# Two 64-row tiles for the first projection, earlier input of the next quad, and a new written order in a conv, attention and Fourier network

## The reference

```
# conv(x), twice, with its own weights each time:
r  = sigmoid(mean_over_positions(x) @ Wr + br)         # 4 mixing weights per image
h  = relu(bn1(x @ sum_e r_e Wpw_e + ...))              # 24 -> 96 channels
h  = relu(bn2(depthwise_3x3(h, sum_e r_e Wdw_e) + ...))
x  = bn3(h @ sum_e r_e Wpwl_e + ...) + x               # 96 -> 24
# then on tokens, each with a layer norm over channels before it:
t += linear_attention(ln(t))                           # no softmax: q (k^T v)
t += ffn(ln(t))                                        # operands rounded to fp8, sums to f16
t += fourier_layer(ln(t))                              # 24 -> 48, fft over tokens, per-channel mix, relu, ifft, 48 -> 24
t += ffn(ln(t))
```

## Time and profile before

| | us |
|---|---|
| median of 3 runs (lowest, highest) | 2447.91 (2443.51, 2450.33) |
| profiled execution | 2448.76 |
| its span | 2447.0 |
| mean granted TensorE clock | 0.903 |

### The profile page before, as it was taken

One profiled execution on the slowest core, in us unless ns is written; L12 is line 12 of the kernel. 1 busy time (PEld: TensorE's weight loads), 2 busy tenths in 40 slices (PEclk: granted clock), 3 DMA queues, 4 the chain that ended last, 5 costly groups with the idle time before them and its releaser, 6 DMA issues.

```text
span 2447.0 us, 48861 instructions
## 1 busy us (share of the span) xinstructions
PE 2087.6 (85%) x19720; PEld 1234.5 (50%) x19720; DVE 1924.6 (79%) x3745; ACT 1583.8 (65%) x2704; POOL 114.6 (5%) x290
## 2 busy tenths in 40 slices
PE   3777988999979989999789987898889998887865
PEld 2233433664446634665347634376347644663753
DVE  4986988799949999699959996698978999366253
ACT  3344447775777677765777666776767667767544
POOL 0000000000000000000000000000000000000000
PEclk9887989999979999999989997899999999987765
DMA  5001000100020000100020002000010000000000
GB/s 147 1 1 21 1 1 5 18 2 1 1 40 2 2 1 15 28 2 1 1 40 2 2 1 41 1 2 1 1 32 2 2 1 1 22 2 1 21 1 20
DMA packets 108591, 29.62 MB, mean 12 GB/s; under 512 B 104144, under 2 KB 104272, under 8 KB 107984
## 3 DMA queue, kind: packets, MB, share of 16 engines
q1 hardware_dynamic: 108368, 26.50, 5.3%
HBM read 16.85 MB, written 9.63 MB: 11 GB/s over the span
## 4 chain that ended last, share of the span: by engine, by line
DVE 40%; PE 36%; ACT 13%; issue 7%; SPq 3%; DMA 1%; ACTq 0%; DVEq 0%
DVE acc L1505 19%; PE P L757 7%; PE P L738 5%; PE P L972 4%; DVE SQ L1670 3%; PE P L1064 3%; SPq L598 3%; DVE arena L1654 3%; PE P L909 2%; DVE arena L1670 2%; PE P L779 2%; DVE roots L1670 2%; PE P L806 2%; PE P L985 2%; DVE T L1521 1%
## 5 line engine op out<-in xcount | busy, mean ns | idle before, releaser
L1505 DVE SCALAR_TENSOR_TENSOR acc<-H,Dm,acc 128x784 f32<-128x784 f32 x1024 | 999.2, 1029 | 30.7 <-ACT acc L1140 30.3
L738 PE MATMUL P<-T,Wk 112*128 112x448 f32 (+1 forms) x768 | 385.7, 593 | 55.7 <-ACT H L1133 32.2
L757 PE MATMUL P<-H,diag 64*64 64x392 f32 x4608 | 404.5, 501 | 15.5 <-DVE T L1521 12.4
L1133 ACT ACTIVATE H<-P,biasA 128x448 f32<-128x448 f32 (+1 forms) x384 | 237.3, 622 | 206.0 <-PE P L738 182.7
L757 PEld LDWEIGHTS P<-H,diag 64*64 64x64 f32 x4608 | 174.9, 135 | 228.7 <-issue 191.1
L738 PEld LDWEIGHTS P<-T,Wk 112*128 112x128 f32 x768 | 130.8, 200 | 172.2 <-ACT H L1133 104.1
L1163 ACT ACTIVATE acc<-P,biasT 128x392 f32<-128x392 f32 x128 | 71.7, 584 | 128.8 <-PE P L757 128.8
L1140 ACT ACTIVATE acc<-H,Dm 128x784 f32<-128x784 f32 x128 | 121.6, 950 | 8.1 <-PE P L779 5.8
L1169 ACT ACTIVATE acc<-acc,biasA 128x784 f32<-128x784 f32 x128 | 118.4, 948 | 10.7 <-DVE acc L1505 10.4
L997 PE MATMUL P<-pack_b,arena 128*96 128x112 f32 x928 | 112.3, 268 | 10.6 <-DVE roots L1670 4.6
L972 PEld LDWEIGHTS P<-pack_b,arena 113*64 113x64 f32 x1792 | 112.7, 216 | 16.8 <-issue 7.6
(11 more groups left out here) (209 smaller groups left out, 3630.0 us busy)
## 6 DMA issues: line engine op xcount, KB each, us to landing
xin<-in_x SPq DMA_DIRECT2D x224, 42.0 KB, 2.3
out_y<-arena SPq DMA_DIRECT2D x8, 1176.0 KB, 6.1
pack_b<-in_pack_b SPq DMA_DIRECT2D x1, 3870.5 KB, 17.5
arena<-in_pack_s SPq DMA_DIRECT2D x1, 1584.0 KB, 8.6
pack_a<-in_pack_a SPq DMA_DIRECT2D x1, 1084.0 KB, 5.3
pack_i<-in_pack_i SPq DMA_DIRECT2D x1, 320.0 KB, 3.2
arena<-in_pack_k SPq DMA_DIRECT2D x1, 192.0 KB, 3.4
```

The costliest lines, as they stand in the source:

```text
L738: pe.matmul(conv_rows(slice(0, 128), HB[(NP * s + e) % len(HB)], n), Wk1[:, 128 * j:128 * (j + 1)], image_rows(T[q % 3], a, n), start=True ...
L757: last = pe.matmul(conv_rows(slice(64 * h, 64 * (h + 1)), CVB + r, HH), diag[64 * r:64 * (r + 1), tap, :], H1[64 * r:64 * (r + 1), slot(s, ...
L1133: act.activation(H1[:, slot(s, j), o:o + n, 1:1 + HW], conv_rows(slice(0, 128), HB[(NP * s + e) % len(HB)], n), ACT.Relu, bias=biasA[:, j, ...
L1505: ins = ve.scalar_tensor_tensor(a, H1[:, slot(s, j), r:r + SR, c:c + HW], Dm[:, j, tap:tap + 1], a, ALU.mult, ALU.add)
```

## The change

Seven edits:
1. `hidden`: tile 0 takes only rows 0 to 63 of the contraction (images 0 and 1) and tile 2 only rows 64 to 111 (images 2 and 3); the rows left out are zero in the weights. Both matmuls of a pair are issued in one step and write two banks. Tile 1 keeps all 112 rows. The pieces are taken in the order tile 0, tile 2 (8 rows each), tile 0, tile 2 (the rest), tile 1.
2. Banks: hidden pieces, and the input of quads after the first, have banks 0 and 5. Back has 6 and 7 left, the router's result is in bank 0.
3. There are four T buffers, so the copy to T waits for the output of quad q - 4.
4. The input's sums have a tile of their own (`part_in`), and the input transposes no longer wait for the end of the quad before; they wait for its `h1_ready`. The wait for that end now stands on DVE before the mixing of the weights.
5. The first quad's input groups 4 to 6 are loaded ahead of the packs "s" and "b".
6. PE's taps of a strip are three steps, not one.
7. All strings of `TURNS` are new. POOL waits for its own last memset in middle, and a scratch for DMAs is halved.

```diff
--- before.py
+++ after.py
 TURNS = {
...
     "tensor": (
-        "c15 d1 c9 d1 c4 d3 c2 m1 c2 d4 c1 d3 c9 d1 c8 d3 m1 c1 d1 c1 d1 c3 m1 c2 m1 d2 c1 m1 d1 m1 d1 m3 d1 "
...
+        "c13 d1 c1 d1 c1 d1 c3 d2 c1 d2 c1 d1 c2 d1 c2 d2 c1 d9 c5 d1 c1 d1 c2 d1 c3 d1 c1 m1 d1 c1 m1 d4 c2 "
...
     "scalar": (
-        "c8 m1 c9 d1 c1 d1 c7 d1 c1 d1 c2 d2 c2 d1 c3 d1 c5 d4 c2 d4 c14 d1 c3 d3 c2 d2 c5 d2 m1 c8 d4 m2 c1 "
...
+        "c19 d1 c3 d1 c1 d2 c2 d1 c3 d1 c3 d1 c1 d1 c4 d2 c3 d2 c1 d4 c1 m1 c15 d2 c2 d1 c2 d1 c2 m1 c1 d2 c2 "
...
     "vector": (
-        "c3 m1 c20 d1 c2 d1 c18 d1 c2 d1 c12 d2 c10 d2 c23 d2 c16 d1 c3 d1 c13 d1 c2 d1 c10 d2 m1 c1 m2 c2 m4 "
...
+        "c22 d2 c18 d2 c16 d1 c1 d1 c10 d2 c3 m1 c21 d2 c14 d2 c17 d2 c12 d2 c2 m1 c1 m6 c1 m1 c25 d1 c2 d1 c3 "
...
-    XG = 4
-    MB, CB = (3, 4), (0, 1, 2)
+    XG, TB = 4, 4
+    MB, CB, HB = (3, 4), (0, 1, 2, 5), (0, 5)
...
-    BB = (5, 6, 7)
+    BB = (6, 7)
...
+    def input_banks(q):
+
+        return CB if q == 0 else HB
+
     def hidden_banks(q, L):
 
-        return CB[:1] if q > 0 else CB[:1] + MB + BB if L == 0 else CB[:1] + BB
+        return HB if q > 0 else HB + MB + BB if L == 0 else HB + BB
...
-        Ts = [sb(f"T{n}", [R, TOK]) for n in range(3)]
+        Ts = [sb(f"T{n}", [R, TOK]) for n in range(TB)]
...
-        part = sb("part", [R, 8])
+        part, part_in = sb("part", [R, 2 * NS]), sb("part_in", [R, NCK])
...
+        LGB, CVB = 0, 1
 
...
-        pieces = ((0, 0), (0, 1), (2, 0), (2, 1), (TJ, 0), (TJ, 1))
+        pieces = ((0, 0), (2, 0), (0, 1), (2, 1), (TJ, 0), (TJ, 1))
...
                 sp.dma_start(pack_t[key], packs[key]).then_inc(par_loaded[key].sem, 16)
             load(0, range(XG))
-            for key in ("a", "s", "b"):
+            sp.dma_start(pack_t["a"], packs["a"]).then_inc(par_loaded["a"].sem, 16)
+            load(0, range(XG, NCK))
+            for key in ("s", "b"):
                 sp.dma_start(pack_t[key], packs[key]).then_inc(par_loaded[key].sem, 16)
             for q in range(NQ):
-                load(q, range(XG, NCK))
+                if q > 0:
+                    load(q, range(XG, NCK))
                 if q + 1 < NQ:
                     load(q + 1, range(XG))
...
                 pool_e.memset(bdw[2][:, 0:MR], 0.0).then_inc(ones_ready.sem, 1)
+                pool_e.wait_ge(ones_ready.sem, ones_ready.at(q, 2))
                 yield from shift_terms(q, normM, 1)
...
                     if g == 0 and not first(q):
-                        pe.wait_ge(cv_added.sem, cv_added.at(q, 0))
-                    if g >= 3:
-                        pe.wait_ge(in_evac.sem, in_evac.at(q, g - 2))
+                        pe.wait_ge(h1_ready.sem, h1_ready.at(q, 0))
+                    if g >= len(IB):
+                        pe.wait_ge(in_evac.sem, in_evac.at(q, g - len(IB) + 1))
                     for s in range(BPG):
                         o = RC * (BPG * (n % XG) + s)
-                        last = pe.transpose(P[0:R, g % 3, BLK * s:BLK * (s + 1)], xin[:, o:o + R], par["ident"][0:BLK, 0:BLK])
+                        last = pe.transpose(P[0:R, IB[g % len(IB)], BLK * s:BLK * (s + 1)], xin[:, o:o + R], par["ident"][0:BLK, 0:BLK])
                     last.then_inc(in_tp.sem, 1)
...
                 last.then_inc(lg_psum.sem, 1)
 
             def hidden(q, L):
-                HB = hidden_banks(q, L)
+                banks = hidden_banks(q, L)
                 for s in range(NS):
                     for e, (j, k) in enumerate(pieces):
                         a, n, _ = piece_rows(s, k)
-                        yield
-                        if s == 0 and e == 0:
-                            pe.wait_ge(cw_ready.sem, cw_ready.at(q, L + 1))
-                        else:
-                            pe.wait_ge(h1_ready.sem, h1_ready.at(q, max(NP * L * NS, NP * (L * NS + s) + e + 1 - len(HB))))
-                        pe.matmul(conv_rows(slice(0, 128), HB[(NP * s + e) % len(HB)], n), Wk1[:, 128 * j:128 * (j + 1)],
-                                  image_rows(T[q % 3], a, n), start=True, stop=True).then_inc(h1_psum.sem, 1)
+                        pair = j != TJ
+                        if not pair or j == 0:
+                            yield
+                            if s == 0 and e == 0:
+                                pe.wait_ge(cw_ready.sem, cw_ready.at(q, L + 1))
+                            else:
+                                pe.wait_ge(h1_ready.sem, h1_ready.at(q, max(NP * L * NS, NP * (L * NS + s) + e + 1 + pair - len(banks))))
+                        rows = slice(32 * j, 32 * j + 64 - 8 * j) if pair else slice(0, R)
+                        pe.matmul(conv_rows(slice(0, 128), banks[(NP * s + e) % len(banks)], n), Wk1[rows, 128 * j:128 * (j + 1)],
+                                  image_rows(T[q % TB][rows, :], a, n), start=True, stop=True).then_inc(h1_psum.sem, 1)
...
                 for tap in range(NTAP):
                     dy, dx = tap // 3, tap % 3
+                    if tap and dx == 0:
+                        yield
                     for r in range(2):
                         for h in range(2):
                             last = pe.matmul(conv_rows(slice(64 * h, 64 * (h + 1)), CVB + r, HH), diag[64 * r:64 * (r + 1), tap, :],
...
+                IB = input_banks(q)
                 for g in range(NCK):
                     yield
-                    if g == 0 and q >= 3:
-                        act.wait_ge(ot_psum.sem, ot_psum.at(q - 2, 0))
+                    if g == 0 and q >= TB:
+                        act.wait_ge(ot_psum.sem, ot_psum.at(q - TB + 1, 0))
                     act.wait_ge(in_tp.sem, in_tp.at(q, g + 1))
-                    act.activation(by_token_block(T[q % 3])[:, BPG * g:BPG * (g + 1), :],
-                                   P[0:R, g % 3, 0:CK].rearrange("p (s n) -> p s n", s=BPG),
-                                   ACT.Copy, accum_out=part[:, g:g + 1]).then_inc(in_evac.sem, 1)
...
-                link(ve.tensor_reduce(pool[:, :], part[:, 0:(NCK if L == 0 else 2 * NS)], AX.X, ALU.add), q, "conv")
+                link(ve.tensor_reduce(pool[:, :], part_in[:, :] if L == 0 else part[:, :], AX.X, ALU.add), q, "conv")
...
                 yield
                 ve.wait_ge(rw_ready.sem, rw_ready.at(q, L + 1))
+                if L == 0 and not first(q):
+                    ve.wait_ge(cv_added.sem, cv_added.at(q, 0))
 
...
```

More of the change, by code:

```diff
@@ L422, in build @@
         P = ctx.enter_context(nc.psum_tensor("P", [128, 8, 512], F32))
-        LGB, CVB = 2, 1
+        LGB, CVB = 0, 1
         def image_rows(t, r0, n):
@@ L806, in layer_norm @@
                         pe.matmul(P[0:R, cen[c % NC], 0:CK], par["cen"][0:R, :],
-                                  T[q % 3][:, CK * c:CK * (c + 1)], start=True, stop=True).then_inc(norm.cen_psum.sem, 1)
+                                  T[q % TB][:, CK * c:CK * (c + 1)], start=True, stop=True).then_inc(norm.cen_psum.sem, 1)
                     if c >= 1:
@@ L1063, in output_transposes @@
                     for s in range(BPG):
-                        last = pe.matmul(P[0:BLK, FB[g % BN], RC * s:RC * (s + 1)], by_token_block(T[q % 3])[:, BPG * g + s, :],
+                        last = pe.matmul(P[0:BLK, FB[g % BN], RC * s:RC * (s + 1)], by_token_block(T[q % TB])[:, BPG * g + s, :],
                                          par["rest"][0:R, :], start=True, stop=True)
@@ L1108, in copy_in @@
             def copy_in(q):
+                IB = input_banks(q)
                 for g in range(NCK):
                     yield
-                    if g == 0 and q >= 3:
-                        act.wait_ge(ot_psum.sem, ot_psum.at(q - 2, 0))
+                    if g == 0 and q >= TB:
+                        act.wait_ge(ot_psum.sem, ot_psum.at(q - TB + 1, 0))
                     act.wait_ge(in_tp.sem, in_tp.at(q, g + 1))
-                    act.activation(by_token_block(T[q % 3])[:, BPG * g:BPG * (g + 1), :],
-                                   P[0:R, g % 3, 0:CK].rearrange("p (s n) -> p s n", s=BPG),
-                                   ACT.Copy, accum_out=part[:, g:g + 1]).then_inc(in_evac.sem, 1)
+                    act.activation(by_token_block(T[q % TB])[:, BPG * g:BPG * (g + 1), :],
+                                   P[0:R, IB[g % len(IB)], 0:CK].rearrange("p (s n) -> p s n", s=BPG),
+                                   ACT.Copy, accum_out=part_in[:, g:g + 1]).then_inc(in_evac.sem, 1)
             def conv(q, L):
-                HB = hidden_banks(q, L)
+                banks = hidden_banks(q, L)
                 yield
@@ L1132, in relu1 @@
                         act.wait_ge(acc_ready.sem, acc_ready.at(q, L * NV + 2 * (s - 2) + j // 2 + 1))
-                    act.activation(H1[:, slot(s, j), o:o + n, 1:1 + HW], conv_rows(slice(0, 128), HB[(NP * s + e) % len(HB)], n), ACT.Relu,
+                    act.activation(H1[:, slot(s, j), o:o + n, 1:1 + HW], conv_rows(slice(0, 128), banks[(NP * s + e) % len(banks)], n), ACT.Relu,
```

(12 more changed lines are left out.)

## The result

The changed kernel takes 2414.1 us (median of four, 2404.5 to 2420.7), the kernel before 2449.1 us in the same session: ratio 0.986, 95% interval 0.982 to 0.990. That is 35 us faster, where 75 were forecast. The profiled execution took 2420.7 us with a span of 2418.8; before, 2448.8 and 2447.0. It was the slowest of the four, so its trace shows 28 of the 35 us; the same kernel was profiled again as after_again, with a span of 2407.7.

A forecast was written before the change was run, and what follows sets the result against it. Bounds: PE full and DVE nearly full in long stretches, conv dependencies at quad changes. From 2448.8 us: start -15, changes of quads -60, pairs -19, order of pieces +4, back's bank +15, giving 2374 us; range 2285 to 2448.

The forecast's parts named there:

- rival 3: Hidden matmul pairs don't run beside each other; PE gains nothing and pays 41 us of shape changes: 2408 us, chance 0.04.
- Rival 1: Quad changes return little, their work only moving into stretches where PE is full; 10 instead of 60: 2424 us, chance 0.16.
- The start, -15: Quad 0's input groups load earlier, the seventh at 19.5 us; saves 15 us, between 7 and 22.
- its 7.9 us: Delay of the first taps by `setup_rest` on DVE, expected to cost the same at the second conv: nothing won or lost.
- The changes of quads, -60: Seven windows, a quad's last add to the next quad's first DVE tap, shrink; 60 us saved, bounds 10 and 109.
- Wrong if the windows shrink and the quads' period does not: Sign that would refute the forecast: shorter windows between quads without a shorter period per quad.
- The pairs, -19: Two 64-row hidden matmuls run beside each other; net 52 us of PE, 0.36 of it counting: 19 us saved (0 to 52).
- the price of broken taps: PE's strip taps split into steps: 77 broken blocks at 0.2 us of shape changes, 15 us of PE.
- The order of pieces, +4: First strip: tile 0's second piece waits for two relus, first centre tap 0.6 us later, seven times: 4 us lost.
- Back's lost bank, +15: Back's ffn down to one hidden bank, its Fourier layer to two banks: 15 us lost, between 0 and 160.
- rival 4: Back's two banks make PE stand 0.3 us per group, 160 us: slower, 2519 us; break-even 0.17 us; chance 0.12.

The follow-up runs named there:

- before_loads: Kernel before with only the new order of loads (quad 0's last three input groups ahead of packs s and b): 2435.5 us, 0.996.
- full_rows: Changed kernel with the outer tiles' first projections on all 112 rows, so no pairs: 2422.7 us, 0.991; with a searched order 2411.8 us.
- The uncoupling with a searched order: Kernel before plus fourth T buffer, part_in, later wait on adds, new loads, three-step taps; old banks, no pairs, order from the second search: 2409.4 us, 0.986.
- replan runs: Orders from the first search, by replay with mean durations: changed kernel 2413.4 us, bank5_drain 2391.1 us, kernel before 2493.6 us.
- order2 runs: Orders from a second search, also counting handovers and shape changes: changed kernel 2397.9 us, bank5_drain 2365.8 us, kernel before 2458.2 us.
- bank5_drain: Changed kernel with bank 5 given back to the back stage of quad 6, beside which no conv runs: 2403.9 us, 0.983.
- after_order2: Changed kernel's code with an order from the second search, counting handovers and shape changes: 2397.9 us, 0.981.
- bank5_order2: bank5_drain with an order from the second search, counting handovers and shape changes: 2365.8 us, 0.967.
- one_tap_step: Changed kernel with a strip's nine taps in one step of PE's order, the two freed steps left empty behind it: 2551.3 us, 1.045.

## Why the prediction was right or wrong

The direction was right, the size wrong: 2414 is inside the range and 40 us above the forecast. By the number it lies between rivals 3 (2408) and 1 (2424); the trace rules out 3, and 1 fits in part.

- **The start, -15.** Right in its mechanism. The seventh group came at 20.7 us (19.5 forecast), the first tap 21 us earlier, near the bound of -22. 10 us are the loads' (before_loads); the other 11 came with the new order, in which `setup_rest` has moved. The forecast said that it would cost its 7.9 us elsewhere; quad 0's body grew by 2 (158 to 160).
- **The changes of quads, -60: the step that failed.** The windows shrank by 113 us and the bodies between them grew by 71: 42 are left, of which 10 are the pairs', so some 32 where 60 were taken. The step took the idle time that PE can give in a window, 57 us less 15, and more for the clock, as a gain that stays. That idle time did fall, by 38, but PE's idle time outside the windows rose by 40. "Wrong if the windows shrink and the quads' period does not" is what happened in quads 3 to 6. Rival 1 named the place. Its reason was that PE is full in the bodies; the sums above speak rather for DVE, which the forecast held to be the looser bound: they hold 57 us more of DVE's work, most of it pushed out of the windows (42) and the start (12), while the bodies of full_rows, with 40 to 51 us more of PE's work than the two traces of the changed kernel, are only 1 to 12 us longer (1880 against 1879 and 1868). No run takes DVE's work alone out of the bodies, so this is argued. The uncoupling with a searched order ends 26 us below before_loads (2409 and 2436) and 49 below the kernel before with a searched order (2458, which has the old loads); both differences also hold the taps in three steps.
- **The pairs, -19: mechanism right, half the size.** A pair takes 0.96 us to the next start with 448 columns and 0.86 with 392, as worked out (0.75 or 0.66 and 0.2 for the shape); rival 3 is out. Without the price of broken taps, which full_rows pays too, the working has PE saving 93 - 26 = 67 us. By the timeline a pair of 448 columns saves 0.64 us, yet PE's busy time fell by only 42 to 52. The mean granted clock was 0.898 and 0.901 with the pairs, 0.911 without; by an estimate from these numbers (2057.1 x 0.898 / 0.911 = 2028, to be held against 2099.5) busy time at a like clock would be some 70 us less. Of what was saved, 10 us reached the end in the kernel's own order and 14 in a searched one. Shape changes rose by 311 (686 to 997), where the working had 128 x 2 and 77 x 2, 410. The term charged the broken tap blocks and missed what the order makes of the breaks: without them, 139 us more under this order.
- **The order of pieces, +4.** No run shows it alone.
- **Back's lost bank, +15: mis-placed.** The idle time before back's ffn copies rose to 44.7 us, where 30 was forecast. That before the Fourier layer's matmuls rose from about 40 to 60 us over all quads, 0.04 us a group, so rival 4 (0.17 to break even) is out. But the bank costs where back stands alone, in the drain: the layer of quad 6 grew by 17 us, of which the bank given back there returns 6 to 9 with the order as it is, 15 and 11 with the two searched ones (119.5 to 104.7 in the replan runs, 115.1 to 103.9 in the order2 runs). The whole kernel gains 8, 22 and 32 us by it. Of the 32 (2398 to 2366) not all is the bank's: the drain shrinks by 21 and the windows by 13, which the bank of quad 6's back does not touch.
- **The drain, 0 in the sum, +34 measured.** The sum spoke of no stretch behind quad 7's conv. That conv ends 63 us earlier, the kernel 28, and 22 us more of PE's work stands in a stretch in which PE idles a quarter of the time (102 of 378 us). 7 to 10 of the 34 us are the bank's in this order (bank5_drain). The rest is the order's at least in part: with another order the drain is 369 without the bank (after_order2) and 348 with it and still shorter windows (bank5_order2).

By the measured terms: 20.8 at the start, 41.6 from the windows net of the bodies (10 of them the pairs'), less 34.3 in the drain: 28.1 us, the difference of the spans. The changes of quads fell short by some 28 us, the pairs by 9, and the drain took 34 where 15 stood in the sum for the bank and 4 for the pieces; the start gave 6 more. How much of what the windows gave any order could keep stays open: windows and bodies together are 2045 us before, 2004 after, 1991 in after_order2 and 1980 in bank5_order2.

## What to carry to other kernels

Where engines take steps in a written order, removing a wait need not shorten anything until the order uses it, and here the idle time removed in one place appeared in another: forecast the busy and idle time of each engine over the whole period, not over the window, and ask which engine has to do what is pushed out. Ask of each shared buffer or bank that is taken away where its user stands alone, the last stage above all: it cost nothing beside a conv here, and went to the end there. Before a difference between two codes is put down to the code, vary the order of both: it is worth as much as the change (13 to 50 us here, 38 for bank5_drain), and a search can serve one code better than the other.

## What the runs showed of the hardware

PE's busy time is not a property of its instructions alone. The changed kernel was busy on PE for 2057.1 us in one execution and 2047.6 in another, with mean granted clocks of 0.898 and 0.901. one_tap_step runs the same matmuls, with fewer changes of shape, and PE is busy for 53 us longer than in the first:

```profile
PE 2110.6 (83%) x19720; PEld 1232.0 (48%) x19720; DVE 1943.9 (76%) x3745; ACT 1592.9 (63%) x2702; POOL 116.1 (5%) x290
```

PE idles 433 us in it instead of 362, and its mean granted clock is 0.864. bank5_order2 idles 344 us at 0.909 and is busy for 36.5 us less. In these three traces an order that makes PE wait pays a second time in the clock. Over all traces of this case the ends fit (322 to 324 us idle go with 0.911 to 0.913), but the middle scatters: 354 to 365 us idle go with anything from 0.897 to 0.912. The clock is granted unevenly: 0.52 in the window into quad 3, near the lower of its two levels (1.2 of 2.4 GHz), and 1.00 in the one into quad 7.

Two 64-row tiles of 128 columns that write two banks do run beside each other: four f32 instructions of 448 columns take 0.96 us to the next start, change of shape and all, and the same four on 112 rows (full_rows) 1.60.
